# Filler products on the tensor engine before the first gate product, the first power in two halves, and new orders for the first block

## The reference, cut to what matters

```python
xn = layernorm(x)                                    # eps 1e-5
# attention: 16 heads of 32, chunks of 128, decay s per head
h = rmsnorm(xn) * qkv_norm_w
qkv = h @ ternary(qkv_w).T                           # scale is 1 / mean|w|
o = scale * (((q @ k.T) * mask) @ v + (q * lam) @ S) # S: state carried from chunk to chunk
S = lam_T * S + (k * lam_rev).T @ v
a = rmsnorm(rmsnorm(o) * norm_w) * proj_norm_w @ ternary(proj_w).T
# feed-forward, hidden size 2048
f = (silu(xn @ w_gate.T) * (xn @ w_up.T)) @ w_down.T
out = x + a + f
```

## Time and profile before

| | us |
|---|---|
| median of 3 runs (lowest, highest) | 1362.96 (1362.71, 1363.41) |
| the profiled execution | 1361.45 |
| its span, first to last instruction | 1359.7 |
| PE busy in the span | 1334.2 |
| DVE, ACT, POOL busy | 924.6, 486.5, 67.5 |
| mean granted TensorE clock | 1.000 |

### The profile page before, as it was taken

One profiled execution on the slowest core, in us unless ns is written; L12 is line 12 of the kernel. 1 busy time (PEld: TensorE's weight loads), 2 busy tenths in 40 slices (PEclk: granted clock), 3 DMA queues, 4 the chain that ended last, 5 costly groups with the idle time before them and its releaser, 6 DMA issues.

```text
span 1359.7 us, 21928 instructions
## 1 busy us (share of the span) xinstructions
PE 1334.2 (98%) x8332; PEld 721.3 (53%) x8332; DVE 924.6 (68%) x1886; ACT 486.5 (36%) x915; POOL 67.5 (5%) x88
## 2 busy tenths in 40 slices
PE   5899999999999999999999999999999999999999
PEld 3455555555455554555545555555545555455554
DVE  6988995576655766657766677657775576755655
ACT  7964633233233332333323233223332233232331
POOL 5600000000000000000000000000000000000000
DMA  8242234113431145211351113510145112431121
GB/s 314 83 142 67 87 73 120 26 32 67 111 88 28 30 79 124 53 32 40 71 140 35 29 40 70 148 40 26 38 85 132 32 30 49 94 94 32 32 48 47
DMA packets 193767, 98.72 MB, mean 73 GB/s; under 512 B 127104, under 2 KB 179328, under 8 KB 192000
## 3 DMA queue, kind: packets, MB, share of 16 engines
q1 hardware_dynamic: 193376, 97.30, 28.3%
q10 hardware_dynamic: 288, 0.01, 0.0%
HBM read 34.35 MB, written 8.39 MB: 31 GB/s over the span
## 4 chain that ended last, share of the span: by engine, by line
PE 94%; DVE 3%; ACT 1%; DMA 1%; SPq 1%; issue 1%; POOL 0%; DVEq 0%; POOLq 0%
PE bank L517 89%; PE bank L559 2%; PE bank L586 1%; PE bank L588 1%; DVE wg_lo L1292 0%; SPq L935 0%; DMA xin<-x 0%; ACT wg_lo L1142 0%; DMA k_stack<-k_parts 0%; DVE arena L861 0%; DMA q_stack<-q_parts 0%; DVE arena L747 0%; DVE xt L748 0%; DVE wd_lo L1292 0%; DVE wu_lo L1292 0%
## 5 line engine op out<-in xcount | busy, mean ns | idle before, releaser
L517 PE MATMUL bank<-wd_hi,arena 128*128 128x512 f16 x1024 | 317.0, 379 | 0.0
L517 PE MATMUL bank<-xt,wg_hi 128*128 128x512 f16 x1024 | 306.5, 381 | 3.6 <-ACT ql L728 1.6
L517 PE MATMUL bank<-xt,wu_hi 128*128 128x512 f16 x1024 | 304.6, 379 | 0.0
L517 PE MATMUL bank<-xt,wg_lo 128*128 128x512 f16 x512 | 195.0, 381 | 0.0
L517 PE MATMUL bank<-wd_lo,arena 128*128 128x512 f16 x512 | 194.0, 379 | 0.0
L517 PE MATMUL bank<-xt,wu_lo 128*128 128x512 f16 x512 | 194.0, 379 | 0.0
L517 PEld LDWEIGHTS bank<-wd_hi,arena 128*128 128x128 f16 x1024 | 100.2, 98 | 115.3
L789 DVE TENSOR_TENSOR sm<-bank,mask 128x512 f32<-128x512 f32 x128 | 88.1, 688 | 105.4 <-PE bank L559 105.3
L517 PEld LDWEIGHTS bank<-xt,wu_hi 128*128 128x128 f16 x1024 | 99.0, 98 | 104.4 <-issue 0.5
L517 PEld LDWEIGHTS bank<-xt,wg_hi 128*128 128x128 f16 x1024 | 98.2, 98 | 103.5 <-issue 4.6
L673 ACT ACTIVATE sm_hi<-sm 128x512 f16<-128x512 f32 x128 | 80.1, 626 | 193.5 <-DVE sm L789 193.5
(11 more groups left out here) (200 smaller groups left out, 1492.2 us busy)
## 6 DMA issues: line engine op xcount, KB each, us to landing
k_stack<-k_parts SPq DMA_DIRECT2D x192, 64.0 KB, 2.2
q_stack<-q_parts SPq DMA_DIRECT2D x192, 64.0 KB, 2.2
arena<-x SPq DMA_DIRECT2D x8, 1024.0 KB, 5.9
out<-arena SPq DMA_DIRECT2D x32, 256.0 KB, 2.4
xin<-x SPq DMA_DIRECT2D x30, 256.0 KB, 4.5
stage<-up_t SPq DMA_DIRECT2D x4, 1024.0 KB, 5.3
stage<-down_t SPq DMA_DIRECT2D x4, 1024.0 KB, 4.9
stage<-gate_t SPq DMA_DIRECT2D x3, 1024.0 KB, 4.8
```

The costliest lines, as they stand in the source:

```text
L517: last = e.matmul(dst, a, b, start=start and n == 0, stop=stop and n == len(lhs) - 1)
```

## The change

Four things change, all in block 0 or ahead of it.

1. **Filler products.** DVE's first instruction fills `ht[0][:, 0, :]` (128x512 float16) with ones. PE multiplies this tile by itself into the bank of the scores (128x128 by 128x512, as a G product), and nothing reads the results: 8 times at the start, 4 after each of the four tiles of x has landed, 6 after the first variance, 12 ahead of WT 1, 6 ahead of G 0; 48 in all.
2. **The power in two halves.** POOL raises 128x4 elements (for the layer norm) as soon as DVE has the first variance, and 128x4 more (for the RMS norm) three DVE operations later. N4 waits for the first (`s_rs0` at 1), HX for both.
3. **New orders in the first block** on all five engines, none in the steady blocks. In PE's list FX 0 comes ahead of WT 0, WT 2 and WT 3 ahead of FT 0, FT 3 ahead of G 4, SO 0 behind G 4 (it stood behind G 2), V 1 behind G 7. In ACT's list the FX items are spread between WA 0, WA 1 and WH 0,0; WH 0,1 and 0,2 precede SA 0; SA 2 is behind G 0, and WH 1,2 is ahead of it. In DVE's list SS and SO 0 go behind the splits WC 2,0, 2,1 and 3,0. POOL takes MS ahead of RD 5 and RD 6.
4. **Semaphores**: `s_warm` is new; `s_var0` and `s_rs0` count to 2.

The heads of the four lists and the code (the rest of the lists is reordered in the same manner):

```diff
     "PE": [
-        ('WT', 0), ('FX', 0), ('FX', 1), ('FX', 2), ('FX', 3), ('WT', 1), ('G', 0), ('U', 0), ('G', 1), ('U', 1), ('G', 2),
-        ('SO', 0), ('FT', 0), ('WT', 2), ('FT', 1), ('WT', 3), ('U', 2), ('G', 3), ('U', 3), ('FT', 2), ('G', 4), ('SO', 1),
-        ('U', 4), ('G', 5), ('WT', 4), ('FT', 3), ('U', 5), ('WT', 5), ('G', 6), ('U', 6), ('K', 0), ('Q', 0), ('V', 0),
-        ('V', 1), ('SC', 0, 0), ('KT', 0), ('G', 7), ('O', 0, 0), ('OX', 0, 0), ('SC', 0, 1), ('Q', 1), ('K', 1), ('KV', 0),
+        ('FX', 0), ('WT', 0), ('FX', 1), ('FX', 2), ('FX', 3), ('WT', 1), ('G', 0), ('U', 0), ('G', 1), ('U', 1), ('WT', 2),
+        ('G', 2), ('U', 2), ('WT', 3), ('G', 3), ('FT', 0), ('FT', 1), ('U', 3), ('FT', 2), ('FT', 3), ('G', 4), ('SO', 0),
+        ('U', 4), ('WT', 4), ('G', 5), ('U', 5), ('SO', 1), ('G', 6), ('WT', 5), ('U', 6), ('K', 0), ('Q', 0), ('V', 0),
+        ('G', 7), ('SC', 0, 0), ('KT', 0), ('V', 1), ('O', 0, 0), ('OX', 0, 0), ('SC', 0, 1), ('Q', 1), ('K', 1), ('KV', 0),
     "ACT": [
-        ('WA', 0), ('WA', 1), ('WH', 0, 0), ('FX', 0), ('FX', 1), ('FX', 2), ('FX', 3), ('SA', 0), ('SA', 1), ('SA', 2),
-        ('WH', 0, 1), ('WH', 0, 2), ('WH', 1, 0), ('WH', 0, 3), ('WH', 1, 1), ('G', 0), ('SA', 3), ('WH', 1, 2), ('SA', 4),
-        ('WH', 1, 3), ('UH', 0), ('SA', 5), ('G', 1), ('WA', 2), ('WA', 3), ('UH', 1), ('FT', 0), ('G', 2), ('WH', 2, 0),
-        ('WH', 2, 1), ('WH', 3, 0), ('WH', 3, 1), ('FT', 1), ('G', 3), ('SA', 6), ('UH', 2), ('UH', 3), ('FT', 2), ('WA', 4),
-        ('G', 4), ('EL', 0), ('EM', 0), ('WA', 5), ('G', 5), ('UH', 4), ('UM', 0), ('UM', 1), ('UM', 2), ('UM', 3),
-        ('UM', 4), ('UM', 5), ('UH', 5), ('FT', 3), ('K', 0), ('G', 6), ('Q', 0), ('WH', 4, 0), ('WH', 4, 1), ('WH', 5, 0),
+        ('WA', 0), ('FX', 0), ('WA', 1), ('FX', 1), ('WH', 0, 0), ('FX', 2), ('FX', 3), ('WH', 0, 1), ('WH', 0, 2),
+        ('SA', 0), ('SA', 1), ('WH', 1, 0), ('WH', 0, 3), ('WH', 1, 1), ('WH', 1, 2), ('G', 0), ('WA', 2), ('WH', 1, 3),
+        ('SA', 2), ('UH', 0), ('G', 1), ('SA', 3), ('SA', 4), ('WA', 3), ('G', 2), ('SA', 5), ('UH', 1), ('WH', 2, 0),
+        ('WH', 2, 1), ('WH', 3, 0), ('FT', 0), ('FT', 1), ('G', 3), ('SA', 6), ('WA', 4), ('FT', 2), ('UH', 2), ('FT', 3),
+        ('WH', 3, 1), ('G', 4), ('UH', 3), ('EL', 0), ('EM', 0), ('G', 5), ('WA', 5), ('UM', 0), ('UM', 1), ('UM', 2),
+        ('UM', 3), ('UM', 4), ('UM', 5), ('UH', 4), ('UH', 5), ('K', 0), ('G', 6), ('Q', 0), ('WH', 4, 0), ('WH', 4, 1),
     "DVE": [
-        ('S4', 0), ('N4', 0), ('WT', 0), ('WC', 0, 0), ('FX', 0), ('FX', 1), ('FX', 2), ('FX', 3), ('WT', 1), ('WC', 0, 1),
-        ('WC', 1, 0), ('WC', 1, 1), ('WC', 0, 2), ('WC', 0, 3), ('U', 0), ('QN', 0), ('HX', 0), ('WC', 1, 2), ('WC', 1, 3),
-        ('UL', 0), ('SS', 0), ('U', 1), ('HX', 1), ('HX', 2), ('HX', 3), ('SO', 0), ('WT', 2), ('WT', 3), ('FT', 0),
-        ('UL', 1), ('U', 2), ('WC', 2, 0), ('WC', 2, 1), ('WC', 3, 0), ('FT', 1), ('U', 3), ('WC', 3, 1), ('UL', 2),
-        ('UL', 3), ('RD', 0), ('SO', 1), ('FT', 2), ('U', 4), ('RD', 1), ('WT', 4), ('U', 5), ('HD', 0), ('WT', 5),
-        ('UL', 4), ('WN', 0), ('UL', 5), ('FT', 3), ('K', 0), ('U', 6), ('Q', 0), ('WC', 4, 0), ('WC', 4, 1), ('WC', 5, 0),
-        ('SC', 0, 0), ('V', 0), ('WC', 5, 1), ('SL', 0, 0), ('KT', 0), ('V', 1), ('SC', 0, 1), ('Q', 1), ('SL', 0, 1),
+        ('S4', 0), ('N4', 0), ('FX', 0), ('WT', 0), ('FX', 1), ('FX', 2), ('WC', 0, 0), ('FX', 3), ('WT', 1), ('WC', 0, 1),
+        ('WC', 1, 0), ('WC', 1, 1), ('WC', 0, 2), ('WC', 0, 3), ('WC', 1, 2), ('U', 0), ('QN', 0), ('HX', 0), ('UL', 0),
+        ('U', 1), ('WC', 1, 3), ('WT', 2), ('HX', 1), ('HX', 2), ('WT', 3), ('HX', 3), ('U', 2), ('UL', 1), ('FT', 0),
+        ('FT', 1), ('SS', 0), ('WC', 2, 0), ('WC', 2, 1), ('U', 3), ('WC', 3, 0), ('SO', 0), ('UL', 2), ('FT', 2),
+        ('WC', 3, 1), ('U', 4), ('UL', 3), ('RD', 0), ('RD', 1), ('U', 5), ('WT', 4), ('SO', 1), ('HD', 0), ('FT', 3),
+        ('WT', 5), ('WN', 0), ('UL', 4), ('UL', 5), ('K', 0), ('U', 6), ('Q', 0), ('WC', 4, 0), ('WC', 4, 1), ('WC', 5, 0),
+        ('V', 0), ('SC', 0, 0), ('WC', 5, 1), ('SL', 0, 0), ('V', 1), ('KT', 0), ('SC', 0, 1), ('Q', 1), ('KV', 0), ('K', 1),
     "POOL": [
-        ('S4', 0), ('RD', 2), ('RD', 3), ('RD', 4), ('RD', 5), ('RD', 6), ('MS', 0), ('NR', 0), ('ST', 0), ('NR', 1),
+        ('S4', 0), ('RD', 2), ('RD', 3), ('RD', 4), ('MS', 0), ('RD', 5), ('RD', 6), ('NR', 0), ('ST', 0), ('NR', 1),
         ('ST', 1),
     # POOL, S4
-                    e.wait_ge(s_var0, 1)
-                    e.tensor_tensor(rs_0, var_0[:, 0:2, :], mhalf_0.rearrange("p (a c) -> p a c", a=2), ALU.pow)\
-                        .then_inc(s_rs0, 1)
+                    for k in range(2):
+                        e.wait_ge(s_var0, k + 1)
+                        e.tensor_tensor(rs_0[:, k, :], var_0[:, k, :], mhalf_0[:, 0:TPB], ALU.pow).then_inc(s_rs0, 1)
     # PE
+            e.wait_ge(s_warm, 1)
+            def keep_busy(n):
+                for _ in range(n):
+                    e.matmul(b_sc[:, :], ht[0][:, 0, 0:P], ht[0][:, 0, :], start=True, stop=True)
+            keep_busy(8)
+            for c in range(TPB):
+                e.wait_ge(ld_first[c], 16)
+                keep_busy(4)
+            e.wait_ge(s_var0, 1)
+            keep_busy(6)
             e.wait_ge(s_ident, 3)
             def first_item(it):
                 kind, n = it
+                if it == ("WT", 1):
+                    keep_busy(12)
+                        if (blk, it) == (0, ("G", 0)):
+                            keep_busy(6)
                         tensor_item(e, it, blk)
     # DVE
+            e.memset(ht[0][:, 0, :], 1.0).then_inc(s_warm, 1)
             e.memset(state1[:, :], 1.0)
-                    link(e.tensor_scalar(var_0[:, 0, :], mv_0[:, :, 1], LN_EPS, None, ALU.add))
+                    e.tensor_scalar(var_0[:, 0, :], mv_0[:, :, 1], LN_EPS, None, ALU.add).then_inc(s_var0, 1)
+                    e.wait_ge(s_var0, 1)
                 elif kind == "HX":
+                    e.wait_ge(s_rs0, 2)
```

More of the change, by code:

```diff
@@ L400, in build @@
     s_inverse, s_clip_pool, s_total = sem("beta_inverse"), sem("clipped_pool"), sem("beta_read")
+    s_warm = sem("warm_tile")
     s_spread, s_allmax = sem("piece_max_spread"), sem("piece_max_read")
```

## The result

The changed kernel takes 1364.96 us (median of 17 runs, 1364.37 to 1366.45) against 1362.71 us for the kernel before, timed beside it (17 runs, 1361.38 to 1364.38): ratio 1.0017, 95% interval 1.001 to 1.0025. It is 2.3 us slower, where I had forecast 1.8 us faster, with a range that ended 0.9 us above the kernel before. The profiled executions, from which all rows are read, took 1364.74 us, with a span of 1362.7, and 1361.45 and 1359.7 before: they lie 3.3 us apart, the medians 2.3.

A forecast was written before the change was run, and what follows sets the result against it. PE, busy 98%, bounds the kernel, decided in the first 85 us; the smaller of PE's lead (1.9) and DVE's (2.0), taken as 1.8 us, gives 1361.2 us against the median 1362.96; range 1358.9 to 1363.9.

The forecast's parts named there:

- Steps 1 to 3: Up to G 1: earlier power, fillers costing nothing, ACT's new order to the first Silu; lead at G 1 1.9 us.
- rival of the low clock in the fillers: Slow fillers delay FX 0 to 14.5 us and G 1 to 27.9; time 1364.6 us; chance 0.10.
- Step 4: PE from G 1 to U 4: splits undisturbed by POOL save 1.5 to 2.4 us; U 4 at 45, not 46.55.
- Step 5: Late SO 0: three POOL chunks in 7.7 us, tables at 58.7, DVE past HD at 59.2 instead of 61.21.
- rival of the late tables: POOL's three chunks take 10.5 us, tables at 61.5: no gain, 1363.2 us; chance 0.15.
- Step 6: From HD to 85 us: same DVE work reordered, K 0 at 62.3, lead of 1.8 us kept.
- The lead of PE: PE's 1.9 us lead from G 1 on, taken as still there at 85 us.
- U 0's gap: Sign in the first block: PE waits ahead of U 0, from 20.7 to 21.4 us, for split WC 1,0.
- MS at 53: Sign on POOL: MS starts at 53.1 us, after three rounding chunks.
- the item behind HD at 59.2: Sign on DVE: the item following HD starts at 59.2 us, against 61.21 before.
- K 0 at 62.3: Sign on PE: K 0 starts at 62.3 us instead of 64.67, after RD 5 and UM 5.
- the limit of 55.5: Failure sign on POOL: the prediction would be wrong if MS began behind 55.5 us.

The follow-up runs named there:

- FT 3 early: The changed kernel with DVE's FT 3 moved from behind HD to behind FT 2, so PE's WT 5 gets its bank sooner: ratio 1.0017.
- the control of the WN trial: The kernel before with WN split, all but its last small operation placed ahead of U 5 on DVE: ratio 1.0008.
- WN in the wait: The changed kernel with FT 3 behind FT 2 on DVE, and WN ahead of HD there: ratio 1.0023.
- WN split: The changed kernel with FT 3, SO 0 and RD 5 early, and all but WN's last operation ahead of WT 3 on DVE: ratio 0.9991, median 1361.48 us.

## Why the prediction was wrong

**Steps 1 to 3 were right but for one small term.** N4 at 10.1 (I had 10.0), G 0 at 18.17 in 2.6 us (18.1, 2.6), the table load at 22.38 (22.5), G 1 at 24.50 (24.6), so the lead of 1.9 us was there. The term is the rise of the clock in the fillers, which came at about 7.4 us and not at 6.3. Five slow fillers instead of three behind tile 0's landing held FX 0 until 11.1 (10.7), where it starts at 10.72 without fillers; so they did not cost nothing there, but G 0 did not feel it. The rival of the low clock in the fillers is out.

**Step 4 was right.** U 4 at 45.30 (45.0), released by WC 3,0, which was done at 45.2 and not at 44.4; the two splits WC 2,0 and 2,1 in 2.47 us, POOL's start at 45.62 (45.4), DVE's waits of 1.75 and 1.48 us (1.8 and 1.4).

**Step 5 failed in one term.** The three chunks of POOL took 9.6 us, not 7.7: 3.7, 3.0 and 2.9, the first beside WC 3,1 and DVE's small tiles, the others beside RD 0 and RD 1. I had taken POOL's price from the earlier trace rows where DVE left it alone, for all but 0.2 us; for the first chunk the bound of 4.0 was nearer, and the other two cost 0.4 to 0.5 more than alone. MS began at 55.20 and its tables were there at 60.80, not 58.7. DVE's side was right: RD 0 and RD 1 took 5.9 us (6.3), HD's last operation ended at 58.86 (59.2) and then waited 2.02 us. The lead of 2.0 us at this point shrank to 0.3 (60.89 against 61.21). That is my rival of the late tables, but not its end: it gave no gain, and the kernel lost.

**Step 6 failed in its first sentence**, "The same DVE work as before (...) follows in another order; DVE had no idle time in it". The work is the same, its price is not. POOL's new list puts MS ahead of RD 5 and RD 6, so RD 6 moved from 51.2, where it stood ahead of MS, to 63.2, beside WN: 5.52 us instead of 3.26. And FT 3 behind HD opens a new wait: FT 3 clears the bank of WT 5, PE sat in front of it for 4.1 us, and DVE waited 0.47 us for WT 5 in turn. By DVE's rows the sum against my forecast is 1.7 (60.89 instead of 59.2), 0.6 (that wait, and 0.1 in FT 3's row ahead of it) and 2.3 (WN), 4.6 us together. From a forecast of 2.0 us ahead this makes 2.6 behind; measured at the K 0 product are 2.5.

**Which part counts is shown by the runs, not by the sum.** Taking PE's wait for ht away changed nothing. Moving RD 6 or WN changed the place of the loss. Only the early SO 0 with RD 5 ahead of MS took it away, 0.23% or 3.1 us; with both, and FT 3 early, the other new orders stand as they were, and the kernel is level with the one before (0.9994, with 1 inside the interval). So the cause is that the change postponed all of POOL's work by ten microseconds (45.62 against 35.02) and put RD 5 and RD 6 behind MS, into the stretch of 45 to 67 us in which DVE has little slack. How much each of the two steps holds is not settled by the runs. The saving I had booked in step 4, undisturbed splits, was real: 1.8 us over the three (2.47 and 1.28 us where 3.45 and 2.06 stood). It was paid back later with more, 0.9 us in RD 0 and RD 1 (5.94 us where 1.38 and 3.67 stood) and 2.3 in WN.

**The lead of PE was not worth what I gave it.** It even grew: G 6 started at 54.78 instead of 58.52. But DVE's HD, which waits for the tables, is a meeting of PE, DVE and POOL, and PE stood still ahead of it. What the fillers added was lost earlier still, since ACT releases G 6 at 54.7 with or without them. I had taken the smaller of PE's lead and DVE's, which was right, and sized DVE's wrong.

The places where it would be seen to fail were well chosen: U 0's gap, G 1, the splits came true; MS at 53, the item behind HD at 59.2 and K 0 at 62.3 (66.15) did not. Nor did the steady stretch: from 85 to 194 us PE is busy 106.72 of 109.00 us, where it was 108.81, so that new waits stand behind 85 us, the one at SC 1,0 among them. MS at 55.20 lay just inside the limit of 55.5 that I had set, which was too lenient. The rivals were too mild: none of the three had WN beside RD 6, and the slowest of them lost its time in the fillers.

## What to carry to other kernels

An item that is moved takes the price of its new neighbours. Before pricing a new order, write down for two engines that slow each other, as DVE and POOL do here, what runs beside what, in both orders; if the work of the one is postponed, look where its cost goes before booking a saving. A lead ahead of a meeting of several engines is worth only what the last of them gains. And the longest new wait of a profile need not be the loss: where its removal changes nothing, the engine may only wait for the next thing, as PE did for UM 5.

## What the runs showed of the hardware

**A small operation can wait for a whole long one.** HD's last operation, 128x16, took 0.29 us in the control of the WN trial, where POOL was idle, and took 2.01 us when POOL's 128x2048 began 0.01 us behind it; it ended 0.03 us after POOL's. WN's 128x512 product of two SBUF tiles takes 0.68 us and 2.37 beside POOL. Not every operation pays: beside RD 5 and RD 6, DVE's 128x1 operations kept their 0.15 us and WN's reduction over 128x512 its 0.68 (61.06 to 62.54 in the kernel with FT 3 early). The Trainium skill, page "SBUF — State Buffer", section "SBUF: two separate sides", calls the shared pair an exclusive lock: whichever instruction starts first has it for its whole length, and the other "fully blocks". These rows agree with a wait for a whole instruction, though by the rows the 128x16 operation was the one that began first. The prediction had applied the rule to RD 0 and RD 1 alone.

**The clock after an idle stretch.** After the changed kernel's PE had waited 4.1 us, the granted clock fell once U 6 had begun, in the busy time by stretch (length, then PE, PEld, DVE, ACT, POOL, clock, DMA):

```profile
61.60:64.00 2.40, 2.37 (x8) 1.05 (x9) 1.74 (x10) 0.83 (x1) 2.22 (x3) 0.58 0.00 0
64.00:65.00 1.00, 1.00 (x4) 0.32 (x3) 0.93 (x3) 1.00 (x3) 1.00 (x1) 0.50 0.00 0
65.00:66.00 1.00, 1.00 (x5) 0.41 (x4) 0.96 (x2) 0.27 (x1) 0.92 (x2) 0.79 0.00 0
66.00:67.00 1.00, 1.00 (x10) 0.80 (x9) 1.00 (x1) 0.00 (x0) 1.00 (x1) 1.00 0.00 0
```

0.50 is the lower of the two levels, 1.2 GHz. It cost U 6 about 1.7 us (4.27 us for 12 products from 61.88 to 66.15, where others take 2.59), and the kernel nothing, as the run with FT 3 early shows. The length of the wait does not decide it alone. With FT 3 early PE waited 3.09 us ahead of K 0, with WN in the wait 3.41, and the clock stayed at 1.00. With WN split it waited only 2.05 us, and the clock read 0.50 from 66 to 68 us; Q 0 took 2.98 us there instead of 1.89.

**The fall can come late.** Without fillers PE had only transposes and two small products up to 15.5 us, the transposes at half pace (eight in 1.91 us, where eight take 1.04 in the changed kernel later on). Then it waited 2.58 us. Yet G 0's first products ran at the full pace and the low pace followed after 1.4 us (18.09 to 19.5), until about 22.7; the granted clock reads 0.50 from 19.5 to 22.7. In the kernel before G 0 was at the low pace from its start. The two cases differ by when the transposes ran and by the wait ahead of G 0; which of these decides was not tried.
